# Values copied by ScalarE and completed by GpSimd, two more half batches lerped, in a chain of attention cells

## What is computed

```python
x = L0_attn_x
x = x + _L0_attn_ref(_layernorm(x), ...)     # time mixing
x = x + _L0_ffn_ref(_layernorm(x), ...)      # six cells
...
# time mixing
k = (x * mix_k + last_x * (1 - mix_k)) @ Wk.T      # v and r alike
wkv = _wkv_scan(exp(k), v, td)                     # den = den*td + k;  num = num*td + k*v;  num/den
out = sigmoid(r) * wkv @ Wo.T
...
# cell c of 6, H = 8 heads of 16 channels, D = 128
q = ew[c, 0] * (nodes[in_q] @ We[eq] + be[eq])
k = ew[c, 1] * (nodes[in_k] @ We[ek] + be[ek])
v = ew[c, 2] * (nodes[in_v] @ We[ev] + be[ev])
o = _mha(q, k, v, Wq[c], Wk[c], Wv[c], Wo[c])      # softmax attention over 1024 positions
nodes[c] = act_w[c] * o + q
```

## Times and profile before

| | us |
|---|---|
| runs of the kernel | 2209.26 median, 2208.71 to 2211.22 |
| profiled execution, its own time | 2205.83 |
| its span, first to last instruction | 2204.0 |
| TensorE busy | 2165.4 (98%) |
| VectorE busy | 2048.1 (93%) |
| ScalarE busy | 1796.8 (82%) |
| GpSimd busy | 561.3 (25%) |
| TensorE's clock granted, mean | 0.995 |

### The profile page before, as it was taken

One profiled execution on the slowest core, in us unless ns is written; L12 is line 12 of the kernel. 1 busy time (PEld: TensorE's weight loads), 2 busy tenths in 40 slices (PEclk: granted clock), 3 DMA queues, 4 the chain that ended last, 5 costly groups with the idle time before them and its releaser, 6 DMA issues.

```text
span 2204.0 us, 43679 instructions
## 1 busy us (share of the span) xinstructions
PE 2165.4 (98%) x16565; PEld 881.6 (40%) x16565; DVE 2048.1 (93%) x3242; ACT 1796.8 (82%) x3432; POOL 561.3 (25%) x689
## 2 busy tenths in 40 slices
PE   6999999999999999999999999999999999999997
PEld 3534343344344343443443443443443433434432
DVE  6989999999999999999999999999999999999995
ACT  4367888888888888888888888888888888888885
POOL 4451223312503212112113113123022121421313
PEclk9999999999999999999999999999999999999998
DMA  4230323413324224233234133142242242341311
GB/s 121 74 71 27 75 66 68 82 47 87 74 49 100 55 58 85 66 70 82 58 72 82 46 73 80 43 87 67 47 85 57 60 84 57 65 94 48 72 34 44
DMA packets 87537, 149.40 MB, mean 68 GB/s; under 512 B 35146, under 2 KB 49950, under 8 KB 87326
## 3 DMA queue, kind: packets, MB, share of 16 engines
q0 software_dynamic: 28224, 94.13, 20.4%
q1 hardware_dynamic: 59102, 52.46, 9.5%
HBM read 42.36 MB, written 14.91 MB: 26 GB/s over the span
## 4 chain that ended last, share of the span: by engine, by line
PE 92%; DVE 6%; issue 1%; SPq 1%; ACT 0%; POOL 0%; DMA 0%; POOLq 0%; DVEq 0%; ACTq 0%
PE context L662 35%; PE ring L617 32%; PE wide L641 10%; DVE max_neg L1283 2%; PE wide L552 2%; PE wide L524 2%; PE wide L532 2%; PE wide L543 2%; PE wide L557 2%; DVE max_neg L1280 2%; PE context L487 1%; PE ring L455 0%; DVE mixing L1092 0%; PE ring L456 0%; PE ring L430 0%
## 5 line engine op out<-in xcount | busy, mean ns | idle before, releaser
L912 ACT ACTIVATE e_ring<-ring 128x512 f32<-128x512 f32 x3053 | 1602.2, 601 | 270.2 <-PE ring L617 267.2
L1280 DVE TENSOR_REDUCE max_neg<-wide 128x1 f32<-128x512 f32 x1804 | 1133.0, 682 | 62.7 <-PE wide L641 58.9
L641 PE MATMUL wide<-k_aug,q_aug 48*128 48x512 f32 x3072 | 1050.0, 439 | 4.4 <-DVE max_neg L1283 2.4
L617 PE MATMUL ring<-q_aug,k_aug 50*128 50x512 f32 x3053 | 1032.5, 436 | 0.0
L662 PE MATMUL context<-e_ring,v_aug 128*32 128x256 f32 (+1 forms) x9240 | 902.9, 462 | 3.4 <-ACT raw L921 3.3
L1283 DVE TENSOR_REDUCE max_neg<-wide 128x2 f32<-128x1024 f32 x634 | 769.6, 1219 | 26.5 <-PE wide L641 21.2
L617 PEld LDWEIGHTS ring<-q_aug,k_aug 50*128 50x128 f32 x3053 | 490.3, 185 | 707.3 <-ACT e_ring L912 619.9
L641 PEld LDWEIGHTS wide<-k_aug,q_aug 48*128 48x128 f32 x3072 | 499.0, 184 | 23.8 <-DVE max_neg L1283 6.7
L662 PEld LDWEIGHTS context<-e_ring,v_aug 128*32 128x32 f32 x9240 | 184.4, 108 | 414.6 <-issue 291.3
L397 POOL DMA_DIRECT2D src<-node_dram x40 | 22.8, 570 | 638.7 <-DMA rows_dram<-max_turn 638.7
L1407 POOL CAST q_part<-q_part 128x512 fp32r<-128x512 f32 x46 | 28.7, 625 | 373.5 <-DVE max_turn L1302 197.9
(11 more groups left out here) (260 smaller groups left out, 958.9 us busy)
## 6 DMA issues: line engine op xcount, KB each, us to landing
q_aug<-q_part POOLq DMA_DIRECT2D x138, 256.0 KB, 4.1
k_aug<-k_part POOLq DMA_DIRECT2D x138, 256.0 KB, 6.5
src<-node_dram POOLq DMA_DIRECT2D x40, 512.0 KB, 7.5
ctxT<-raw SPq DMA_DIRECT2D x380, 32.0 KB, 1.9
rden_bc<-rden_dram SPq DMA_DIRECT2D x23, 512.0 KB
node_dram<-node_ring SPq DMA_DIRECT2D x16, 512.0 KB, 3.0
q_aug<-rows_dram SPq DMA_DIRECT2D x192, 8.0 KB
node_ring<-in_L_attn_x SPq DMA_DIRECT2D x4, 512.0 KB, 4.9
```

What stands on the lines that cost most here:

```text
L617: e.matmul(bk[:, :], k_aug[first:first + AUG, u % 2, h // 2, chunk * P:(chunk + 1) * P].bitcast(F32R), q_aug[first:first + AUG, u % 2, h / ...
L641: e.matmul(bk[:, :], q_aug[first:first + SPLIT, u % 2, head // 2, q0:q0 + P].bitcast(F32R), k_aug[first:first + SPLIT, u % 2, head // 2, h ...
L912: e.activation(e_ring[:, n % E_SLOTS, :], bank[where["st", n]][:, :], ACT.Exp, scale=EXP_SCALE).then_inc(a_exp, 1)
L1280: e.tensor_reduce(max_neg[:, G % 2, kh, row:row + 1], wide[:, b, :], AX_X, ALU.max, negate=True).then_inc(v_mx, 1)
```

## The change

1. From unit 1 on, ScalarE copies the values out of PSUM into `v_aug` (`evict_v` of the scalar program, in `evict`, behind the exponentials, as keys and queries), and GpSimd adds the constant in place (`add_value_constant`, at the step of the product, after `wait_split`). The bank comes free with ScalarE's copy (`a_v`), the next unit's weighted sums wait for GpSimd (`g_v`). Unit 0's values stay on VectorE.
2. i = 4 and 5 are lerped by GpSimd too, at steps -3 and 6, and four stages of i = 5 come later: the projections of k and v by two steps, that of r and the scan of the denominator by one.
3. At stage GATE GpSimd waits for the transpose of this and of the next step, where a column is due there. For i = 4 (step 11) and i = 5 (step 20) one is.
4. Group 92's context moves are issued at step 754 and no longer at 757.

```diff
-        LERPED = (6, 7)
+        LERPED = (4, 5, 6, 7)
         ON_RING = (TURN, PROJ_K, PROJ_V, PROJ_R, OUT, TURN2)
-        GPSIMD_PRODUCT = (4, 5, 6, 7)
+        GPSIMD_PRODUCT = LERPED
...
-            (-9, -8, -8, -4, -4, -4, -4, -4, 1, 2, 3, 3, 4, 4, 6, 7, 8, 10, 11, 12, 13, 14, 14, 17),
-            (-3, -2, -1, 3, 4, 4, 4, 4, 6, 8, 10, 10, 12, 12, 15, 16, 18, 19, 20, 22, 23, 26, 26, 30),
+            (-9, -8, -8, -4, -3, -3, -3, -3, 1, 2, 3, 3, 4, 4, 6, 7, 8, 10, 11, 12, 13, 14, 14, 17),
+            (-3, -2, -1, 3, 6, 6, 6, 6, 8, 10, 11, 11, 12, 12, 15, 16, 18, 19, 20, 22, 23, 26, 26, 30),
...
-                freed[at] = (v_v, 2 * u + hf + 1)
+                freed[at] = (v_v, hf + 1) if u == 0 else (a_v, 2 * u + hf - 1)
...
-                            e.wait_ge(v_v, 2 * u + 2)
+                            if u == 0:
+                                e.wait_ge(v_v, 2)
+                            else:
+                                e.wait_ge(g_v, 2 * u)
...
+            def evict_v(u, hf):
+                if u >= 2:
+                    e.wait_ge(p_ctx, UC * (u - 1))
+                if u == 1 and hf == 0:
+                    e.wait_ge(p_mt2, IN_VALUES + 1)
+                e.wait_ge(p_v, 2 * u + hf + 1)
+                e.activation(v_aug[:, u % 2, hf * CPB:(hf + 1) * CPB, :, 0:DH],
+                             bank[where["v", u, hf]][:, :].rearrange("p (k h d) -> p k h d", k=CPB, h=H), ACT.Copy).then_inc(a_v, 1)
+
...
+                if kind == "v":
+                    evict_v(unit, hf)
...
-                if nxt == 1 and half == 0 and r in FIRST_V_AT:
-                    evict_v(nxt, FIRST_V_AT.index(r))
...
-                if 1 < nxt < UNITS and r - 1 in V_AT:
-                    evict_v(nxt, V_AT.index(r - 1))
...
+            def add_value_constant(u, hf):
+                c, _ = CELLS[u]
+                values = v_aug[:, u % 2, hf * CPB:(hf + 1) * CPB, :, 0:DH]
+                e.wait_ge(a_v, 2 * u + hf - 1)
+                e.wait_ge(d_bias_in, DMA * (1 if c == 0 else 2))
+                row = v_bias0[:, :] if c == 0 else v_bias[:, c - 1, :]
+                after()
+                signal(e.tensor_tensor(values, values, row.rearrange("p (o h d) -> p o h d", o=1, h=H).to_broadcast([P, CPB, H, DH]),
+                                       ALU.add), g_v)
+
...
+                    if r in v_steps(nxt):
+                        wait_split(s + 1)
+                        add_value_constant(nxt, v_steps(nxt).index(r))
...
+                        if k == GATE:
+                            wait_split(s)
+                            wait_split(s + 1)
                         mix(i, k)
...
+                    if s == STEPS - UC + 18:
+                        move_ctx(GROUPS - 4)
                     G = (s - 21) // NCH
-                    if s % NCH == 5 and 0 <= G < GROUPS and G % GPU == 0:
+                    if s % NCH == 5 and 0 <= G < GROUPS - 4 and G % GPU == 0:
                         move_ctx(G)
-                        if G + 1 != GROUPS - 3:
-                            move_ctx(G + 1)
+                        move_ctx(G + 1)
```

More of the change, by code:

```diff
@@ L168, in build @@
         p_last_den, g_w_last, g_to_values, d_w_last, v_x2b = sems("p_last_den g_w_last g_to_values d_w_last v_x2b")
+        a_v, g_v = sems("a_v g_v")
         d_x, d_x2_out, d_spill = ([sem(f"{n}{b}") for b in range(B)] for n in ("d_x", "d_x2_out", "d_spill"))
@@ L1117, in evict_v @@
                 k0 = hf * CPB
-                if u >= 2:
-                    e.wait_ge(p_ctx, UC * (u - 1))
-                if u == 1 and hf == 0:
-                    e.wait_ge(p_mt2, IN_VALUES + 1)
                 e.wait_ge(p_v, 2 * u + hf + 1)
```

## The result

The changed kernel takes 2187.9 us in the median of four runs (2185.2 to 2188.1), the kernel before beside it 2210.2; the ratio is 0.989 [0.9863, 0.9917]. The forecast was 2187. The profiled execution took 2187.92 us with a span of 2186.0, against 2205.83 and 2204.0 before. So profile against profile it is 17.9 us, not the 22.4 of my sum. The total was right, some of its parts were not, and one was missing.

A forecast was written before the change was run, and what follows sets the result against it. TensorE was taken to pace, with VectorE late in four places. Terms -7.9 - 1.4 - 4.4 - 4.2 + 0.3 - 4.8 = -22.4 us took the profile from 2205.83 to 2183.4, the median to 2187; 8-in-10 range 2179 to 2196.

The forecast's parts named there:

- my sum: Whole kernel: all terms together -22.4 us, taking the profiled 2205.83 us to 2183.4 us.
- (a): Steps 28 and 29, units 1 to 22: moving value evictions off VectorE saves 0.36 us each, -7.9 us.
- Units 20 and 22, -1.4: There VectorE is late for several steps, so both moved evictions count in full: 2.0 us, of which -1.4 taken.
- over four steps before: GpSimd's first value add was said to come over four steps before the VectorE split, so it costs 0.
- (b): Unit 0: lerping i = 4 and 5 saves TensorE matmuls, -2.9 and -1.5, together -4.4 us (bounds -1.5 and -5.7).
- The first lerp wait: Step 8 of unit 0: TensorE would wait 0 to 1.5 us for GpSimd's first lerp of i = 5.
- R1: VectorE keeps pacing unit 0, so (b) and (c) bring 2 us instead of 8.6; time 2193; chance 0.13.
- (c): Unit 0: gate waits for the split; -4.2 us at step 20 (stand 1.1, clock 3.4), +0.3 at step 12.
- R2: Unit 0: GpSimd's lerps come late, TensorE stands over 1.8 us, the clock falls again; time 2198; chance 0.07.
- (d): Last unit: earlier group 92 moves end ScalarE's 2.34 us idle time and the fallen clock, -4.8 us.
- the 3.4 us that I added: Gap between the kernel before's profiled execution and its 2209.26 us median, taking 2183.4 to 2187 us.
- R5: GpSimd's add comes too late for each unit's first weighted product: 110 us more, about 2295; chance 0.03.

The follow-up runs named there:

- experiment 1: Kernel before, with only the second half batch of the values (from unit 1) copied by ScalarE and completed by GpSimd: 2201.9 us, ratio 0.9974.
- experiment 2: Kernel before, with only the first half batch of the values (from unit 1) copied by ScalarE and completed by GpSimd: 2208.1 us, ratio 1.0005.
- Experiment 7: Kernel of experiment 6, with GpSimd's first add behind the power and first half's apply in units following a batch's last cell: 2182.6 us, ratio 0.9884.
- experiment 10: Kernel before, with only i = 4 and 5 lerped too, with their later stages: 2205.7 us in one run.
- experiment 4: Kernel before, with only group 92's context moves issued at step 754 instead of 757: 2206.7 us, ratio 1.0004.
- experiment 6: Changed kernel, with GpSimd's normalising at step 10 waiting for the transpose of step 12's column: 2184.2 us, ratio 0.9892.
- experiment 8: Changed kernel, without the wait for the column's transpose before the adds of the value constant: 2188.4 us, ratio 0.9911.
- experiment 9: Kernel of Experiment 7, with an unused GpSimd operation of two SBUF inputs ahead of step 28's column in units 8 to 22: 2191.99 us, one run.
- experiment 5: Changed kernel run again without edits: 2188.6 us in eight runs (2184.0 to 2202.2), ratio 0.9913.
- experiment 12: Kernel of Experiment 7, with i = 4's last inverse part moved from step 10 to 9 and its gate from 11 to 10: 2184.6 us, ratio 0.9899.

## Why the prediction was right, and where it wasn't

**(a) Values, -7.9: right in mechanism and place.** Experiments 1 and 2 show both. The pairs of steps 28 and 29 gave 8.6 us over 22 units, and the pair behind them 0.05 more in each, 1.1: 9.7 where I had 7.9. Copy and second add cost 0, as said. ScalarE's copy took 0.60 us, less than the 0.69 of the nearest row.

**Units 20 and 22, -1.4: wrong.** The two units together gained 0.36 us (0.07 and 0.29), where my sum has 2 x 0.36 + 1.4 = 2.1 for them. Steps 28 to 31 gave 0.6 us in each, and steps 24 and 25 took 0.45 back in each. The failed step is "of which I take -1.4 since GpSimd's first add now stands ahead of the final normalising". I had priced GpSimd's order and not the meeting: the add starts 0.04 us ahead of VectorE's operation on the variances and holds it up 1.1 us, more than the 0.69 that the moved eviction saved. My sentence that the first add is "over four steps before" a column looked for columns and not for other small operations. Experiment 7 took the add away and found 1.5 of it. The Trainium skill (SBUF — State Buffer; Who interferes with whom) says that a VectorE tensor_scalar in a two-port mode and a GpSimd instruction exclude one another, not only operations with two SBUF inputs; the 1.25 us beside the add and 0.17 without it agree, though no run shows which mode the operation was in. I had carried over only half of the rule.

**(b) Lerps, -4.4: 3.5 measured** (2.4 for i = 4, taken as 2.9; 1.1 for i = 5, taken as 1.5), inside the bounds. The first lerp wait that I had put at 0 to 1.5 us was 0.88. Of the 5.7 us of work 2.2 were lost: 0.9 is the lerp's wait, 0.9 in i = 5 and 0.5 in i = 4 are open (experiment 10). My reason for taking half of i = 5, a full VectorE, isn't shown, so that its size came near is partly luck. Rival R1 had (b) and (c) bring 2 us together, of 8.3 in the sum (its 8.6 leaves out the 0.3 that (c) gives back); they brought 6.8, so R1 is out.

**(c) The gate's wait, -4.2 and +0.3: 3.85 and 0.5.** The stand fell by 1.08 us as said. The rest is clock, and that was luck: the 3.4 us read from the trace were between 1.8 and 5.1 in other executions (experiment 4). Against the units 0 of experiments 1 and 4, with those two draws, the gate's wait is worth 2.1 or 5.1 us in place of 3.3. The clock held afterwards, so R2 fell; the new stands of 0.7 to 0.9 us brought no fall.

**(d) Group 92, -4.8: 4.7.** The mechanism is right, and the size is partly a draw too: with the move steps 24 to 27 take 8.2 us, and without it between 12.0 and 13.1 in six profiles, which makes 3.8 to 4.9.

**What was missing: +3.7 in unit 23.** I had asked which meetings the change makes or ends, and had looked only where the trace of before has a long row (step 20 of unit 0). A near miss has none. It stood there all the same, VectorE's last operation with two inputs and GpSimd's normalising, in the kernel before:

```profile
2129.59 0.18 DVE L1294 TENSOR_TENSOR max_part<-max_all,max_part 128x16 fp32r<-128x16 f32 x1
```

```profile
2129.97 2.36 POOL L1438 TENSOR_TENSOR ctxT<-ctxT,rden_bc 128x1024 f32<-128x1024 f32 x1 [30.71 <-DMA rden_bc<-rden_dram]
```

They pass by 0.2 us, from the end of the one to the start of the other. Of the ten profiles without the wait of experiment 6, six have the meeting: as far as they show, it is a toss in each execution, worth 3.7 us where it was measured in the changed kernel, and I took one side of it for the kernel's own time. The Trainium skill (same page and section) has it that issue order decides who blocks; experiments 8 and 9 agree: 0.05 us behind costs VectorE nothing, 0.8 us ahead costs the rest of the operation. Whether GpSimd, in its turn, was blocked in experiment 8 the rows don't show: its adds took 1.28 to 1.32 us there and 1.28 elsewhere.

**The total.** Units 1 to 22 gave 9.4 us where the sum had 9.3, since what (a) gave above its 7.9 made up for units 20 and 22. Unit 0 gave 6.8 of 8.3, and the meeting took 3.7; step 0 began 0.9 earlier, which is likely to be chance (in experiment 4, which edits only the last unit, it began 1.1 earlier). Together 17.9 instead of 22.4, so my sum was 4.5 too large. That the median still came out was luck, and due to the 3.4 us that I added to get from the profile to the median: they stood for just such chance losses in the kernel before, whose median lay above its profile, while the profile of the changed kernel had its own share in it. Without the meeting, experiment 5's profile is 2183.99, where the sum said 2183.4. (R5's price is slightly off: 110 us over 2187 are 2297 and not 2295. It decides nothing.)

## What to carry to other kernels

Moving work off a nearly full engine paid here only where that engine ended a wait: half of the moved evictions brought all of the gain, the other half none. An operation put on GpSimd must be placed against every small VectorE operation with two SBUF inputs or one like L1042, and letting it wait for the last of them is cheap where nobody needs its result soon: nothing for the adds and the normalising, 0.5 us for the gate at step 12, whose result TensorE was waiting for. Where two engines pass each other by some tenths of a us in the one trace that you have, count it as a toss in the forecast, and close it in the kernel: with one wait and one later add the median was 6 us lower, and the runs lay within 0.7 us (four of them) instead of 18 (eight). The narrow spread isn't shown to be theirs: experiment 12 has both edits too, and its four runs lay within 5.2 us.

## What the hardware showed

A stand of 1.84 to 1.86 us of TensorE was followed by 1.8, 3.4 or 5.1 us of lost clock (three, two and one of six profiles), so a clock loss read from one trace is one draw. Nor does each such stand bring a fall: in the prologue TensorE stands 1.86 or 1.87 us between 32.0 and 33.4 us in every profile, and the granted clock over 31 to 50 us is 1.00 in all of them. And the clock can fall with no stand: in the profile of experiment 2 TensorE was busy for 14 of 14 us and had 0.63 of its clock, which made its step 0 start 4.4 us later than before:

```profile
85.00:99.00 14.00, 14.00 (x38) 7.72 (x38) 10.01 (x22) 1.03 (x3) 4.21 (x5) 0.63 0.13 45
```

A VectorE operation of 4 to 16 columns that starts while a GpSimd operation with two SBUF inputs runs took as long as that still ran: 2.35, 1.25 and 1.14 us in place of 0.17. This holds for the operations with two inputs and for the one on the variances; a transpose that started inside such an operation took its usual 0.21 us (experiment 8).
